# Both expert biases added by VectorE from tables picked by a register, where matmuls added them

## The chip, the cores and the metric

One core of one Trainium2 chip runs the whole program in one launch. The metric is the device time of that launch in microseconds (us); lower is better. A measurement is the median of several executions.

## What is computed

A decoder layer with three parts, each followed by an addition to its input and a layer norm: self-attention with a dynamic convolution, cross attention over 1601 context rows, and a mixture of experts, which is the part that changes. 4 x 512 tokens of width 256 each go to the best two of eight experts:

```python
logits = jnp.einsum('bsd,de->bse', input, Wg)
probs = jax.nn.softmax(logits, axis=-1)
top_vals, top_idx = jax.lax.top_k(probs, TOP_K)          # TOP_K = 2
top_vals = top_vals / jnp.sum(top_vals, axis=-1, keepdims=True)
...
h = jnp.einsum('ebsd,edh->ebsh', xm, W1) + b1[:, None, None, :]   # 256 -> 512
h = jax.nn.relu(h)
y = jnp.einsum('ebsh,ehd->ebsd', h, W2) + b2[:, None, None, :]    # 512 -> 256
out = jnp.sum(y * jnp.moveaxis(scores, -1, 0)[..., None], axis=0)
```

b1 is 8 x 512 and b2 is 8 x 256. Both are non-zero.

## The kernel before

The three parts run one behind the other, each in a block of its own with one hand-written instruction stream for each engine; semaphores set the order between engines, and the order within an engine is that of the code.

**Ahead.** The object `Ahead` loads what the experts need while the cross attention still runs: the gate's weights, the two biases (`b2_raw`, `b1c`) and the raw weights of experts 0 and 1, into two staging buffers (STG = 2). `Ahead.start` is the first thing that SyncE issues in the cross attention; behind it in the same queue stand the loads of the first batch's input, `xa_xh` and `xa_xl`, which TensorE needs for the first query projection.

**Gate and list.** TensorE computes the gate; VectorE picks the two experts of each token, ranks the 4096 assignments and builds a list of 39 blocks (NBK) of 128 rows, each of one expert: `gidx` and `sidx` say which rows to gather and where to scatter, `eidi` says which expert a block has. Its last step releases `list_ready`.

**Weights.** Each float32 weight is split in two parts. ScalarE writes w_hi (`take_weights`), GpSimd writes w_lo for experts 0, 1, 2, 5, 6, 7 and VectorE for 3 and 4 (`low_weights`). When w_lo of an expert is done, its staging buffer is free and SyncE loads the expert after next. Weights 0 to 4 are taken before the blocks, 5, 6 and 7 at blocks 1, 2 and 4.

**Blocks.** GpSimd gathers the rows of block q three blocks ahead and scatters the results. For one block TensorE turns the rows (`turn_x`, L1395), which are split into xb_hi (ScalarE) and xb_lo (VectorE); runs the first layer (L1409, six matmuls of 512 columns, and L1413, one for b1); turns h_f back (`turn_h`, L1420), which is split into h_hi and h_lo; and runs the second layer (L1427, one for b2, and L1431, twelve of 256 columns). Its order is first_layer(q), turn_x(q+1), second_layer(q-1), turn_h(q). The bias matmuls multiply `sel`, a 128 x 128 selector that ScalarE fills for each block (L1492) from `pick`, with `bx`, which holds both biases in two parts. `xb`, `h_f`, `h_hi`, `h_lo` and `sel` have two buffers each. TensorE reads the expert's number from `eidi` into a register (L1401) for the weights' address.

At the end the results come back from `ybuf`, are weighted, added and normalised.

## Time and profile before

| | us |
|---|---|
| median of 3 runs | 1970.57 |
| lowest and highest | 1967.91, 1973.7 |
| the profiled execution | 1969.15 |
| its span, first to last instruction | 1967.4 |
| TensorE busy in it | 1740.5 (88%) |
| VectorE, ScalarE, GpSimd busy | 1136.5, 864.6, 1290.6 |
| mean granted TensorE clock | 0.937 |

All times below are of the profiled execution, counted from its first instruction. Self-attention ends at about 210, the cross attention at about 1710, and the 39 blocks run from 1771 to 1930. Busy shares are means over stages with different limits, so the stages are read one by one: a row of idle time names what the engine waited for, and a DMA row of the timeline shows the time in issue, not in transfer.

### The profile page before, as it was taken

Reading aid. Unit: us, or ns where it says so; the run is one execution under the profiler, and the core shown is the slowest. Engines: PE = TensorE matmul, PEld = TensorE weight load, DVE = VectorE, ACT = ScalarE, POOL = GpSimd, SP = SyncE. Lnnn points to the kernel's source line nnn. Section 1 sums busy time; section 2 is a strip of 40 time slices with the busy share of each in tenths; the row PEclk is TensorE's granted clock in tenths of the full one; section 3 lists DMA queues with packets and bytes.
Section 4 is the critical chain, followed back from the end, with each engine's and each line's share of the span. In section 5 each row is a group of like instructions: output and inputs, shape, how many; then the busy total and the mean of one; then the engine's idle time right before and its main releaser. Section 6 shows DMA issues by size and latency. Waiting matters only on the chain. (4 is left out here: it accounts for less than half of the span.)

```text
span 1967.4 us, 32756 instructions
## 1 busy us (share of the span) xinstructions
PE 1740.5 (88%) x10682; PEld 1217.7 (62%) x10682; DVE 1136.5 (58%) x1993; ACT 864.6 (44%) x1280; POOL 1290.6 (66%) x721
## 2 busy tenths in 40 slices
PE   6554499999989999998999999989999998649992
PEld 5544366666656666665666666656666675347991
DVE  4776455556565656656565656566665555463444
ACT  3222244445444445444444444544544444334443
POOL 3874438677686676686866767677668677636554
PEclk9877699999999999999999999999999999759996
DMA  6001300000200000010000000200000000023224
GB/s 192 2 22 38 113 1 23 1 23 0 76 1 23 1 24 23 0 55 22 22 1 23 2 22 0 76 1 23 22 1 23 16 0 1 19 95 117 71 71 139
DMA packets 38854, 68.09 MB, mean 35 GB/s; under 512 B 4601, under 2 KB 28545, under 8 KB 37697
## 3 DMA queue, kind: packets, MB, share of 16 engines
q1 hardware_dynamic: 34976, 56.12, 8.5%
q0 software_dynamic: 3744, 10.23, 1.6%
q8 instruction: 80, 1.31, 0.3%
q14 instruction: 54, 0.43, 0.1%
HBM read 52.84 MB, written 13.50 MB: 34 GB/s over the span
## 5 line engine op out<-in xcount | busy, mean ns | idle before, releaser
L1034 POOL TENSOR_TENSOR xa_total<-xa_total,xa_pexp 128x1024 f32<-128x1024 f32 (+1 forms) x352 | 858.3, 2438 | 63.8 <-ACT xa_pexp L975 38.8
L1100 DVE TENSOR_REDUCE xa_parts<-ps_ring 128x1 f32<-128x402 f32 x1024 | 531.9, 565 | 267.4 <-PE ps_ring L920 253.7
L975 ACT ACTIVATE xa_pexp<-ps_s 128x1024 f32<-128x1024 f32 (+1 forms) x416 | 426.1, 1026 | 400.7 <-PE ps_s L875 361.6
L889 PE MATMUL ps_pv<-xa_pexp,xa_v 128*64 128x512 f32 (+1 forms) x1664 | 399.8, 604 | 0.0
L920 PE MATMUL ps_ring<-xa_k_hi,xa_q_hi 64*128 64x402 f32 x1024 | 245.1, 376 | 7.2 <-DVE xa_parts L1100 5.0
L889 PEld LDWEIGHTS ps_pv<-xa_pexp,xa_v 128*64 128x64 f32 (+1 forms) x1664 | 106.1, 136 | 181.9 <-issue 141.6
L875 PE MATMUL ps_s<-xa_q_hi,xa_k_hi 64*128 64x512 f32 (+1 forms) x832 | 203.1, 437 | 3.6 <-DVE xa_k_lo L1088 2.7
L1088 DVE TENSOR_TENSOR xa_k_lo<-ps_ring,xa_k_hi 128x402 fp32r<-128x402 f32 (+1 forms) x128 | 73.6, 575 | 218.8 <-ACT xa_k_hi L986 218.8
L920 PEld LDWEIGHTS ps_ring<-xa_k_hi,xa_q_hi 64*128 64x128 f32 x1024 | 149.6, 186 | 78.8 <-issue 23.3
L875 PE MATMUL ps_s<-xa_q_neg,xa_row_one 64*128 64x512 f32 (+1 forms) x832 | 180.8, 393 | 0.0
L1034 POOL TENSOR_TENSOR xa_total<-xa_pexp 128x1024 f32<-128x1024 f32 x32 | 76.4, 2387 | 158.9 <-ACT xa_pexp L975 157.5
L875 PE MATMUL ps_s<-xa_q_lo,xa_k_hi 64*128 64x512 f32 (+1 forms) x832 | 180.1, 393 | 0.0
L875 PE MATMUL ps_s<-xa_q_hi,xa_k_lo 64*128 64x512 f32 (+1 forms) x832 | 179.7, 392 | 0.0
L1010 ACT COPY xa_v<-ps_ring 128x256 f32<-128x256 f32 (+1 forms) x208 | 77.5, 373 | 184.6 <-PE ps_ring L860 182.7
L1115 DVE RECIPROCAL xa_inv<-xa_sums 128x128 f32<-128x128 f32 x128 | 120.0, 941 | 27.5 <-ACT xa_sums L997 27.5
L1056 POOL TENSOR_TENSOR xa_wa_lo<-wa_raw,xa_wa_hi 128x1536 fp32r<-128x1536 f32 x17 | 59.0, 3472 | 110.0 <-ACT xa_wa_hi L1020 110.0
L875 PEld LDWEIGHTS ps_s<-xa_q_hi,xa_k_hi 64*128 64x128 f32 (+1 forms) x832 | 82.6, 182 | 67.2 <-issue 40.3
L860 PEld LDWEIGHTS ps_ring<-xa_wa_hi,xa_ctx_hi 128*128 128x128 f32 (+1 forms) x416 | 62.3, 185 | 63.9 <-issue 60.9
L875 PEld LDWEIGHTS ps_s<-xa_q_neg,xa_row_one 64*128 64x128 f32 (+1 forms) x832 | 92.2, 181 | 14.3
L875 PEld LDWEIGHTS ps_s<-xa_q_lo,xa_k_hi 64*128 64x128 f32 (+1 forms) x832 | 91.8, 181 | 14.0
L1060 POOL TENSOR_TENSOR xa_wb_lo<-wb_raw,xa_wb_hi 128x512 fp32r<-128x512 f32 x16 | 22.0, 1376 | 116.3 <-ACT xa_wb_hi L1023 116.3
L986 ACT CAST xa_k_hi<-ps_ring 128x402 fp32r<-128x402 f32 (+1 forms) x128 | 63.3, 495 | 79.4 <-PE ps_ring L860 79.4
(272 smaller groups left out, 2956.0 us busy)
## 6 DMA issues: line engine op xcount, KB each, us to landing
wa_raw<-in_pack_a SPq DMA_DIRECT2D x17, 768.0 KB, 4.5
ex_raw<-in_pack_e SPq DMA_DIRECT2D x8, 1024.0 KB, 5.8
ctx_raw<-in_ctxT SPq DMA_DIRECT2D x4, 1601.0 KB, 8.7
wb_raw<-in_pack_b SPq DMA_DIRECT2D x16, 256.0 KB, 2.6
ex_w_hi<-ybuf SPq DMA_DIRECT2D x8, 512.0 KB, 7.3
sa_xT<-in_xT SPq DMA_DIRECT2D x8, 256.0 KB, 6.3
X<-in_x SPq DMA_DIRECT2D x1, 2048.0 KB, 11.1
x_hi<-sa_x1s_hi SPq DMA_DIRECT2D x16, 128.0 KB, 2.1
```

What stands on the lines that cost most here:

```text
L860: ins = nc.tensor.matmul(out, w, x, start=q == 0, stop=q == len(terms) - 1)
L875: ins = nc.tensor.matmul(ps_s[0:m, t_of(n), h, :], kk[half(h)], qq[half(h), :], start=q == 0, stop=q == 3)
L889: ins = nc.tensor.matmul(ps_pv[half(h), :], v[0:m, t, at:at + XD], pexp[0:m, buf, h, :], start=t == 0, stop=t == MT - 1)
L920: nc.tensor.matmul(ps_ring[:, r, 0:CW], q_hi[p][half(h), q * P:(q + 1) * P], k_hi[p][half(h), KC0[c]:KC0[c] + CW], start=True, stop=True)\
L975: nc.scalar.activation(pexp[0:m, buf], ps_s[0:m, (p * MT + t) % 2], ACT.Exp, scale=XD ** -0.5)\
L986: nc.scalar.copy(k_hi[p][:, KC0[c] + skip:KC0[c] + CW], ps_ring[:, r, skip:CW])\
L1010: nc.scalar.copy(v[0:rows(t), t, :], ps_ring[0:rows(t), r, 0:4 * XD]).then_inc(drained[r], 1)
L1034: nc.gpsimd.tensor_tensor(total[p][0:m], first, pexp[0:m, buf], ALU.add).then_inc(s["add_done"], 1)
L1056: nc.gpsimd.tensor_tensor(wa_lo[:], wa_raw[:], wa_hi[:].bitcast(F32), ALU.subtract)\
L1088: nc.vector.tensor_tensor(k_lo[p][:, cols], ps_ring[:, r, skip:CW], k_hi[p][:, cols].bitcast(F32), ALU.subtract).then_inc(drained[r], 1)
L1100: nc.vector.tensor_reduce(parts[:, h, q, c:c + 1], ps_ring[:, r, 0:CW], AX.X, ALU.max)\
L1115: nc.vector.reciprocal(inv[:, cs], sums[:, cs]).then_inc(s["inv_ready"], 1)
```

## The change

Both biases leave TensorE. Two tables hold them on all 128 partitions: `b1_all` (8 x 512 a partition) and `b2_all` (8 x 256). VectorE reads the block's expert into a register of its own and adds a row of the table as it drains PSUM: `take_h`, which was ScalarE's copy, and `take_y`, which was a copy of VectorE's. `sel`, `pick`, `bx` and their preparation go.

`b1_rows` is a new DRAM tensor with b1 in plain order; four DMAs in `Ahead.start` fill it from the packed weights, one number at a time. `b1_all` is loaded from it at the start of the experts. `b2_all` lies over tables of the gate and is loaded once the list is done; the loads of experts 4 to 7 stand behind it in SyncE's order. `xb_hi`, `xb_lo`, `h_f`, `h_hi` and `h_lo` have one buffer instead of two, and the gate's tables share their room with the blocks'. The second layer now starts when h_hi is done and waits for h_lo before its last third.

```diff
     def start(self, sp, a):
         sp.dma_start(self.wg[:], a["Wg"].rearrange("(k p) e -> p k e", p=P)).then_inc(self.sems["small_in"], 16)
-        sp.dma_start(self.b2_raw[:], a["b2"]).then_inc(self.sems["small_in"], 16)
-        sp.dma_start(self.b1c[:], a["pack_e"][:, :, WW:].rearrange("e p c -> p e c")).then_inc(self.sems["small_in"], 16)
+        for c in range(HC):
+            sp.dma_start(self.b1_rows.rearrange("o (e c p) -> (o e) c p", e=NE, c=HC)[:, c], a["pack_e"][:, :, WW + c], allow_slow_non_contiguous=True)\
+                .then_inc(self.sems["rows_in"], 16)
         for e in range(STG):
             self.load(sp, a, e)
...
         @block.sync
         def _(sp):
+            sp.wait_ge(ahead.sems["rows_in"], 16 * HC)
+            sp.dma_start(b1_all[:].rearrange("p e n -> p (e n)"), ahead.b1_rows.broadcast_to([P, NE * HID]))\
+                .then_inc(s["b1_in"], 16)
             for b in range(B):
                 sp.wait_ge(s["x_done"], NC * (b + 1))
...
-            for e in range(STG, NE):
+            for e in range(STG, STG + 2):
+                lo_done(sp, e - STG + 1)
+                ahead.load(sp, a, e)
+            sp.wait_ge(s["list_ready"], 1)
+            sp.dma_start(b2_all[:].rearrange("p e n -> p (e n)"),
+                         a["b2"].rearrange("(o e) n -> o (e n)", o=1).broadcast_to([P, NE * E])).then_inc(s["b2_in"], 16)
+            for e in range(STG + 2, NE):
                 lo_done(sp, e - STG + 1)
                 ahead.load(sp, a, e)
...
-                pe.wait_ge(s["sel_done"], q + 1)
-                nc.tensor.matmul(ps_h[:, q % 2, :], sel[:, q % 2], bx[:, 0:HID], start=False, stop=True)\
-                    .then_inc(s["h_mm"], 1)
...
             def second_layer(q):
                 e = experts_of[q]
-                pe.wait_ge(s["h_done"], q + 1)
+                pe.wait_ge(s["h_hi_done"], q + 1)
                 need(pe, s["y_copied"], q - 1)
-                nc.tensor.matmul(ps_y[:, q % 2, 0:E], sel[:, q % 2], bx[:, HID:HID + E], start=True, stop=False)
                 terms = [(h, w, c) for h, w in ((h_hi, w_hi), (h_hi, w_lo), (h_lo, w_hi)) for c in range(HC)]
                 for n, (h, w, c) in enumerate(terms):
+                    if n == 2 * HC:
+                        pe.wait_ge(s["h_done"], q + 1)
...
             def take_x(q):
                 act.wait_ge(s["xb_tr"], q + 1)
-                need(act, s["h_mm"], q - 1)
-                nc.scalar.copy(xb_hi[:, q % 2], ps_x[:, q % 2, 0:E]).then_inc(s["xb_hi_done"], 1)
-                need(act, s["y_mm"], q - 1)
-                nc.scalar.copy(sel[:, q % 2], pick[:, q:q + 1].bitcast(F32).broadcast_to([P, P])).then_inc(s["sel_done"], 1)
-
-            def take_h(q):
-                act.wait_ge(s["h_mm"], q + 1)
-                need(act, s["h_tr"], q - 1)
-                nc.scalar.copy(h_f[:, q % 2], ps_h[:, q % 2]).then_inc(s["h_copied"], 1)
+                need(act, s["h_mm"], q)
+                nc.scalar.copy(xb_hi[:], ps_x[:, q % 2, 0:E]).then_inc(s["xb_hi_done"], 1)
...
+            def take_h(q):
+                e = dve.value_load(eidi[0:1, q:q + 1], min_val=0, max_val=NE - 1)
+                experts_of[q] = e
+                dve.wait_ge(s["h_mm"], q + 1)
+                need(dve, s["h_tr"], q)
+                nc.vector.tensor_tensor(h_f[:], ps_h[:, q % 2],
+                                        b1_all[:, bass.ds(e, 1), :].rearrange("p a n -> p (a n)"), ALU.add)\
+                    .then_inc(s["h_copied"], 1)
...
-                nc.vector.tensor_copy(y_sb[:, q % 3], ps_y[:, q % 2, 0:E]).then_inc(s["y_copied"], 1)
-
+                nc.vector.tensor_tensor(y_sb[:, q % 3], ps_y[:, q % 2, 0:E],
+                                        b2_all[:, bass.ds(experts_of[q], 1), :].rearrange("p a n -> p (a n)"), ALU.add)\
+                    .then_inc(s["y_copied"], 1)
+
+            dve.wait_ge(s["b1_in"], 16)
             take_x(0)
             for q in range(NBK):
+                take_h(q)
                 if q + 1 < NBK:
                     take_x(q + 1)
```

SyncE, at the start of the cross attention, before (a row gives the line, the tensors and the shape; b_raw is b2_raw):

```order
L738 DMA ex_wg<-in_Wg 128x2x8
L739 DMA ex_b_raw<-in_b 8x256
L740 DMA ex_b1c<-in_pack_e 128x8x4
L735 DMA ex_raw<-in_pack_e 128x2048 x2
L844 DMA xa_xh<-x_hi 128x1024
L844 DMA xa_xl<-x_lo 128x1024
```

The same place in the changed kernel (b_rows is b1_rows):

```order
L740 DMA ex_wg<-in_Wg 128x2x8
L742 DMA b_rows<-in_pack_e 8x128x1 x4
L737 DMA ex_raw<-in_pack_e 128x2048 x2
L847 DMA xa_xh<-x_hi 128x1024
L847 DMA xa_xl<-x_lo 128x1024
```

The b2 and b1c loads have gone, and four DMAs of 8 x 128 x 1 stand in their place, ahead of the same four loads.

SyncE, from the start of the experts to the return of the results, in the changed kernel (both tables are named ex_b_all; the first is b1_all, the second b2_all):

```order
L1255 DMA ex_b_all<-b_rows 128x4096
L1259 DMA x<-X 128x4x256 x4
L737 DMA ex_raw<-in_pack_e 128x2048 x2
L1265 DMA ex_b_all<-in_b 128x2048
L737 DMA ex_raw<-in_pack_e 128x2048 x4
L1275 DMA ex_w_hi<-ybuf 128x4x256 x8
```

Before, this was the stores of x2 and six weight loads (x6) in a row; now the loads of experts 4 to 7 stand behind b2_all.

VectorE, one block in the steady state, before:

```order
L1660 TENSOR_TENSOR ex_xb_lo<-ps_x,ex_xb_hi 128x256
L1674 COPY ex_y_sb<-ps_y 128x256
L1666 SCALAR_TENSOR_TENSOR ex_h_lo<-ps_t,ex_h_hi 128x512
L1660 TENSOR_TENSOR ex_xb_lo<-ps_x,ex_xb_hi 128x256
L1674 COPY ex_y_sb<-ps_y 128x256
```

And in the changed kernel (TENSOR_LOAD reads the register, ISA rows are register work):

```order
L1645 SCALAR_TENSOR_TENSOR ex_h_lo<-ps_t,ex_h_hi 128x512
L1652 TENSOR_LOAD ex_eidi
L1652 ISA x2
L1656 ISA
L1656 TENSOR_TENSOR ex_h_f<-ps_h,ex_b_all 128x512
L1639 TENSOR_TENSOR ex_xb_lo<-ps_x,ex_xb_hi 128x256
L1666 ISA
L1666 TENSOR_TENSOR ex_y_sb<-ps_y,ex_b_all 128x256
```

The register load and the drain of the first layer stand between h_lo of one block and xb_lo of the next.

## Rows read from the trace of the kernel before

**Rows 1.** The page, busy tenths of TensorE in 40 equal slices of the span.

```profile
PE   6554499999989999998999999989999998649992
```

**Rows 2.** Timeline, TensorE, 195 to 260: start, length, line, tensors, [idle before, releaser].

```profile
229.91 1.22 PE L860 MATMUL ps_ring<-xa_xh,xa_wa_hi 128*128 128x512 f32 x2 [4.75 <-DMA xa_xl<-x_lo]
```

**Rows 3.** Timeline, SyncE's queue, 195 to 245: start and length of the issue.

```profile
213.42 0.41 SPq L740 DMA_DIRECT2D ex_b1c<-in_pack_e  x1
...
214.96 4.27 SPq L844 DMA_DIRECT2D xa_xh<-x_hi  x1
```

**Rows 4.** DMA in 214:217, 217:221 and 215:216; then windows, whose last columns are share and GB/s.

```profile
DMA packets 682, 0.01 MB, mean 4 GB/s; under 512 B 680, under 2 KB 682, under 8 KB 682
...
DMA packets 415, 0.73 MB, mean 181 GB/s; under 512 B 327, under 2 KB 327, under 8 KB 327
...
DMA packets 325, 0.01 MB, mean 5 GB/s; under 512 B 325, under 2 KB 325, under 8 KB 325
...
214.00:217.00 3.00, 0.00 (x0) 0.00 (x0) 2.92 (x2) 3.00 (x3) 2.93 (x1) 0.50 0.11 4
...
222.00:228.00 6.00, 2.35 (x6) 1.83 (x6) 1.29 (x2) 0.49 (x1) 6.00 (x3) 0.50 1.01 415
```

**Rows 5.** Timelines of ScalarE, VectorE and TensorE, 1740 to 1772.

```profile
1748.18 1.90 ACT L1455 CAST ex_w_hi<-ex_raw 128x2048 fp32r<-128x2048 f32 x1 [4.51 <-DMA ex_raw<-in_pack_e]
...
1765.06 0.17 DVE L1646 TENSOR_SCALAR ex_gidx<-ex_wrap 128x39 uint32<-128x39 f32 x1
...
1766.31 4.49 DVE L1558 TENSOR_TENSOR ex_w_lo<-ex_raw,ex_w_hi 128x2048 fp32r<-128x2048 f32 x2
...
1771.39 1.22 PE L1409 MATMUL ps_h<-ex_w_hi,ex_xb_hi 128*128 x2 [1.47 <-DVE ex_xb_lo L1660]
```

**Rows 6.** The tile ex_raw, its eight loads from issue to landing.

```profile
DMA to landing us min/median/max: 4.8/5.8/12.9
```

**Rows 7.** Timeline, all engines, 1851.3 to 1863: one steady block.

```profile
1852.07 0.69 DVE L1666 SCALAR_TENSOR_TENSOR ex_h_lo<-ps_t,ex_h_hi 128x512 fp32r<-128x512 f32 x1 [0.64 <-ACT ex_h_hi L1502]
...
1852.61 0.40 PE L1413 MATMUL ps_h<-ex_bx,ex_sel 128*128 128x512 f32 x1
...
1852.85 0.38 PE L1395 MATMUL ps_x<-ident,ex_xg 128*128 128x128 f32 x2
...
1852.98 0.36 PE L1427 MATMUL ps_y<-ex_bx,ex_sel 128*128 128x256 f32 x1
...
1853.18 0.64 PE L1431 MATMUL ps_y<-ex_w_hi,ex_h_hi 128*128 x4
...
1854.60 0.60 PE L1420 MATMUL ps_t<-ident,ex_h_f 128*128 128x128 f32 x4
...
1855.87 0.69 DVE L1666 SCALAR_TENSOR_TENSOR ex_h_lo<-ps_t,ex_h_hi 128x512 fp32r<-128x512 f32 x1 [0.64 <-ACT ex_h_hi L1502]
```

**Rows 8.** Groups by form, 1811.65 to 1923.02: busy, mean ns of one, idle before.

```profile
L1497 ACT COPY ex_h_f<-ps_h 128x512 f32<-128x512 f32 x30 | 17.6, 588 | 30.6 <-PE ps_h L1413 30.6
...
L1413 PE MATMUL ps_h<-ex_bx,ex_sel 128*128 128x512 f32 x29 | 11.4, 394 | 0.0
```

**Rows 9.** The chain that ended last, 1780 to 1794: start, length, what.

```profile
1780.96 1.90 ACT ex_w_hi L1455
1782.94 4.64 POOL ex_w_lo L1300
1787.72 5.55 DMA ex_xg<-x,ex_gidx
```

**Rows 10.** The chain that ended last, at the last block.

```profile
1927.85 0.70 DVE ex_h_lo L1666
...
1928.60 0.39 PE ps_y L1427
1928.98 1.42 PE ps_y L1431 x12
```

**Rows 11.** TensorE's queue at the register load: ns min, median, max.

```profile
L1401 PEldq TENSOR_LOAD <-ex_eidi x39: 296/302/497, 1769.3 to 1922.2; - x39
```

## What the change should do to the time

> **What bounds the kernel now.** I read the slices of the page first: TensorE is at nine tenths or more through the cross attention, from a tenth of the span to nine tenths of it, and falls off on both sides of that stretch [rows 1]. The change touches nothing inside the stretch, but it touches both of its edges, so I read three places: the DMA queue at the start of the cross attention, the gap between the finished list and the first expert block, and the 39 blocks.
>
> At the start of the cross attention the reader is to see that TensorE has stood still for 4.75 us when it goes on at 229.91, and that what it waited for is the DMA that brings xa_xl [rows 2]. From there on TensorE is nearly full, so whatever delays that DMA delays the end by the same amount. It is the last of seven DMAs that SyncE issues in a row, and its predecessor xa_xh stands 4.27 us in issue: the queue is backed up [rows 3]. The packets tell why. From 214 to 217 the engines are 11% busy and move 4 GB/s in 680 packets under 512 bytes, 327 more follow to 221, and only then does the flow reach 415 GB/s [rows 4]. Those 1007 packets are b1c: 128 x 8 pieces of 16 bytes = 1024.
>
> In the blocks, TensorE has no idle time between 1811 and 1923 (the group at L1413 shows 0.0 of it, as do its others), and a block repeats every 3.80 us, 1852.07 to 1855.87 at the h_lo step [rows 7, 8]. The blocks before that are set by another chain: ScalarE w_hi, GpSimd w_lo, then the gather queued behind it, 1780.96 to 1793.32 and once more to 1807 [rows 9].
>
> **The tiny DMAs at the start of the cross attention.** Removed: one of 8 rows (b2) and b1c with 1024 pieces of 16 bytes. Added: four DMAs from DRAM to DRAM, each 8 x 128 x 1, so 4 x 1024 = 4096 pieces of 4 bytes, in the same place of the same queue, ahead of the two raw loads and of xa_xh and xa_xl. No row shows a 4-byte piece written to DRAM. The nearest row is b1c itself. Its pieces take from 214.0 until the large packets have the engines, about 220.5: 6.5 us, or 6.3 ns a piece. 4096 of them take 26.0 us, which is 19.5 more. The low end is the best stretch of the same pieces: 680 in 3 us is 4.4 ns, so 18.0 - 4.5 = 13.5 more, and if the fastest microsecond, 325 packets, held throughout, 3.1 ns and 9.4 more [rows 4]. Below nothing it can't go: more pieces of the same kind in one queue don't end sooner. The high end is double the time of a piece, 52 - 6.5 = 45.5, for the reason given as a rival. I take **+19.5**, since it is the row's own average, head and tail included. Cover: none. TensorE waits for xa_xl already, and ScalarE, VectorE and GpSimd don't stand in that wait.
>
> The count of 4096 is the shape's, as 1007 of 1024 was b1c's. The Trainium skill says the same (DMA: Bandwidth & Descriptors, "Rules for kernel authors"): a non-contiguous last dimension becomes one descriptor per element. It adds, in "Specifications", that under 512 bytes the engine reads, modifies and writes; no row here prices that for a DRAM target. Both speak against this change, and neither enters the sum.
>
> **The new table loads.** b1_all (2 MB, issued at about 1711) lies ahead of the stores of x2, which are needed only at the gathers, after 1765.23; at 415 GB/s it is gone in 5 us: nothing. Without that cover it would cost those 5. b2_all is another matter. SyncE now waits for the finished list before it issues b2_all, and the load of expert 4 is queued behind it. Before, expert 4's weights had landed by 1748.18, when ScalarE copied them, long before the list (1765.06 + 0.17 = 1765.23) [rows 5]. Now both DMAs start at about 1765.1. One load lands 4.8 us after issue at best; the second 1 MB behind it adds 2.6 at 400 GB/s, and three gathers of 128 KB beside them 1.0 [rows 4, 6]. So expert 4 lands at 1773.5. Behind it stand, in order, w_hi on ScalarE (1.90), w_lo on VectorE (half of 4.49, 2.25) and take_x(0) on VectorE (0.35): TensorE starts block 0 at about 1778.4 where it started at 1771.39 [rows 5, 6]. That is **+7.0**; the two bias rows of VectorE that go (1765.26 to 1766.31) gain nothing, being hidden by this wait. Bounds: +5.9 without the gathers' share, +10 if the load takes the 12.9 of the slowest raw load in the trace. The loads of 5 and 6 follow in the same queue: 5 lands by about 1776 and 6 by 1783, and ScalarE wants them 6 us later than 1780.96 and 1784.8, so they have 8 us to spare.
>
> **The blocks.** L1413 goes: from its start to the next start, 1852.61 to 1852.85, 0.24 us. L1427 goes: 1852.98 to 1853.18, 0.20, of which some is weight load that the next matmul may have to pay; an L1431 step is 0.118 (twelve in 1.42), so 0.12 to 0.20, and I take 0.16 [rows 7, 10]. Blocks 8 to 38 are bound by TensorE: 31 x 0.24 + 32 x 0.16 = **-12.5** (-11.3 to -13.8). Before them, in the two blocks at the slow clock ahead of the w_hi chain, go 0.44 (L1413 at half the clock, so a little under twice its 0.24), 0.24 and 0.2, less 0.1 for the slower drain of h_f, and 0.3 for L1427 at half the clock in block 4: **-1.1** [rows 7]. At the end, the last second layer starts behind h_hi instead of h_lo, whose 0.70 now lies under the first eight matmuls (8 x 0.118), and L1427's 0.39 go: **-1.0** [rows 10].
>
> Does what replaces them stay covered? h_f moves from ScalarE (0.588) to VectorE, where a 128x512 read of PSUM with a second operand takes 0.69 [rows 7, 8]. Counted from the start of a turn_h (1850.80, by the period, to the h_lo at 1852.07): VectorE ends h_lo at 1.96, the next first layer has ended by about 2.0, h_f is done at 2.7, and the next turn_h is due only at 3.4 [rows 7]. The register load ahead of it costs TensorE's queue 302 ns today [rows 11]; on VectorE it stands behind h_lo's issue, under its 0.69. Even if it began only when h_lo has ended, h_f would be done at 3.0 and take_x (0.42) behind it at 3.5, before the 3.76 at which the next first layer is due. The skill gives a floor of about 600 ns for tensor_load (same page, "Latency and other measured facts"); the trace has 302, and the trace decides. Single buffers cost nothing: every wait that they add is for a step of TensorE that its own order already puts ahead. VectorE's work rises to 0.69 + 0.69 + 0.42 + 0.42 = 2.2 us of a 3.4 us block, ScalarE's falls.
>
> **Sum:** 19.5 + 7.0 - 12.5 - 1.1 - 1.0 = +11.9 on the profiled execution's 1969.15, which is 1981.0. That execution lies 1.4 under the median of the three, 1970.57, so by the median **1982.5**, say 1983.
>
> **Rivals.** (1) The pieces take twice as long, because the four new DMAs have 8 rows outermost where b1c has 128, and are spread over half of the 16 engines. For it: b1c's pieces leave the engines 11% busy, so something other than data holds them, and that may be a latency per ring. 64 pieces on each of 16 rings in 6.5 us are 0.10 us each; 512 on each of 8 rings are 52 us: +45.5 at the start, 2009 in all. Against it: the pace of b1c jumps within microseconds, which a fixed latency doesn't explain. The Trainium skill (same page, "Why a DMA increments its semaphore by 16 and not by 1") says that a DMA uses the largest number of engines up to 16 that divides its slowest dimension, which is 8 here and 16 for b1c. (2) The other side, **faster**: the pieces are overtaken or pass at several times b1c's pace. For it: nothing forces the raw loads on idle engines to wait. The blocks' gain nets 7.6 after expert 4's wait, so it decides once the start costs less than 7.6; at no cost the time is 1963. Against it: xa_xh stood 4.27 us in issue behind a quarter of the pieces. (3) The start costs the low bounds, 9.4 to 13.5: 1972 to 1976. (4) The register load and the address work behind it take three times TensorE's 302 ns on VectorE, and begin only behind h_lo: 1.96 + 0.9 + 0.69 + 0.42 = 3.97 against 3.76, 0.1 to 0.2 in each of 31 blocks, so +3 to +6 on the forecast, 1986 to 1989.
>
> **How the numbers follow.** A measurement of this kernel can tell about 0.3%, 5.9 us, from no change: under 1964.7 is faster, over 1976.5 slower. Forecast (and 4 within it) 0.50, rival 1 0.23, rival 3 0.15, rival 2 0.12. Slower: 0.73; within: 0.16; faster: 0.11. The range runs from rival 3 with the other terms at their low ends (9.4 + 5.9 - 13.8 - 2.1 = -0.6, 1970) to rival 1, 2010, and leaves out rival 2 and a tail above.
>
> **What would show it.** TensorE's wait for xa_xl should grow from 4.75 to about 24 us, with some 4350 packets under 512 bytes ahead of it; 50 would be rival 1, 5 rival 2. Expert 4's w_hi should start 8 to 9 us after the list instead of 17 before it, and the first block 13.3 us after it instead of 6.2. Steady blocks should repeat every 3.40 us instead of 3.79; 3.5 would be rival 4. The forecast is wrong above all if a 4-byte piece doesn't cost what a 16-byte piece did.

## The result

The changed kernel takes 2015.0 us (median of 4 runs, 2011.5 to 2015.8) where the kernel before takes 1971.7 (4 runs, 1967.9 to 1973.7): a ratio of 1.0223, 95% interval 1.021 to 1.0235. It is slower by 43 us, and the time lies 5 us above the range that was forecast. The profiled execution took 2015.17 us, with a span of 2013.4; before, 1969.15 and 1967.4.

I lay the two spans side by side at five events that both kernels have. All times are starts unless an end is named, in us from the start of the span; the last two columns are a later experiment, explained below.

| event | before | after | later by | `e12_b2_late` | later by |
|---|---|---|---|---|---|
| first statistics of the expert stage (VectorE) | 1711.35 | 1760.38 | +49.0 | 1706.97 | -4.4 |
| list finished (end of `gidx`) | 1765.23 | 1814.23 | +49.0 | 1761.26 | -4.0 |
| block 0, first layer | 1771.39 | 1826.85 | +55.5 | 1768.33 | -3.1 |
| `turn_x(8)` | 1807.26 | 1863.86 | +56.6 | 1803.49 | -3.8 |
| end of the span | 1967.4 | 2013.4 | +46.0 | 1953.1 | -14.3 |

So 49.0 us were lost before the experts began, 6.5 between the list and block 0, 1.1 in the first eight blocks, and 10.6 were won back by the blocks behind them.

**The start of the cross attention.** The slices of the page show it at once: one slice is 50 us, and TensorE's fifth, at 4 tenths before [rows 1], is empty now.

```profile
PE   6655049999999999999999999999999999646992
```

The timeline of TensorE in the changed kernel (start, length, line, tensors, [idle before, releaser]) is the counterpart of [rows 2]: it goes on at 280.41 instead of 229.91.

```profile
280.41 1.22 PE L863 MATMUL ps_ring<-xa_xh,xa_wa_hi 128*128 128x512 f32 x2 [54.80 <-DMA xa_xl<-x_lo]
```

SyncE's queue in the changed kernel (start and length of the issue), the counterpart of [rows 3], shows what stands ahead of that DMA. The four table DMAs alone hold the queue for 28.81 us, and xa_xl is issued at 252.47.

```profile
213.41 28.81 SPq L742 DMA_DIRECT2D b_rows<-in_pack_e  x4
242.27 6.58 SPq L737 DMA_DIRECT2D ex_raw<-in_pack_e  x2
248.90 3.53 SPq L847 DMA_DIRECT2D xa_xh<-x_hi  x1
252.47 0.88 SPq L847 DMA_DIRECT2D xa_xl<-x_lo  x1
```

The packets of the changed kernel in 214:220, 220:230, 230:240, 240:250 and 250:260, the counterpart of [rows 4]:

```profile
DMA packets 1484, 0.02 MB, mean 4 GB/s; under 512 B 1483, under 2 KB 1483, under 8 KB 1483
...
DMA packets 600, 0.00 MB, mean 0 GB/s; under 512 B 600, under 2 KB 600, under 8 KB 600
...
DMA packets 96, 0.00 MB, mean 0 GB/s; under 512 B 96, under 2 KB 96, under 8 KB 96
...
DMA packets 1724, 0.06 MB, mean 6 GB/s; under 512 B 1717, under 2 KB 1717, under 8 KB 1717
...
DMA packets 529, 0.28 MB, mean 28 GB/s; under 512 B 495, under 2 KB 495, under 8 KB 495
```

They add up to 4391 small packets; the count was forecast (4350). The pace was not: after 1483 in the first 6 us it breaks down, and in ten whole microseconds 96 pass.

**Expert 4 and block 0.** The counterpart of [rows 5], timelines of the changed kernel from 1812 to 1827:

```profile
1814.06 0.17 DVE L1630 TENSOR_SCALAR ex_gidx<-ex_wrap 128x39 uint32<-128x39 f32 x1
...
1814.26 0.33 SPq L1265 DMA_DIRECT2D ex_b_all<-in_b  x1
...
1822.04 1.90 ACT L1456 CAST ex_w_hi<-ex_raw 128x2048 fp32r<-128x2048 f32 x1 [28.63 <-DMA ex_raw<-in_pack_e]
...
1823.97 2.29 DVE L1545 TENSOR_TENSOR ex_w_lo<-ex_raw,ex_w_hi 128x2048 fp32r<-128x2048 f32 x1 [7.54 <-ACT ex_w_hi L1456]
...
1826.85 1.22 PE L1415 MATMUL ps_h<-ex_w_hi,ex_xb_hi 128*128 x2 [2.92 <-DVE ex_xb_lo L1639]
```

The reader sees the chain that the prediction wrote down: the load lands, ScalarE copies w_hi 7.8 us behind the list, VectorE makes w_lo, then xb_lo, and block 0 starts 12.6 us behind the list, where it was 6.2. But the first gather is late too: `turn_x(0)`, which uses its rows, starts at 1823.27, 9.0 us behind the list, and before at 1769.26, 4.0 behind it.

**A steady block.** Timelines of TensorE and VectorE in the changed kernel, the counterpart of [rows 7]:

```profile
1877.81 0.38 PE L1401 MATMUL ps_x<-ident,ex_xg 128*128 128x128 f32 x2
1877.95 0.72 PE L1436 MATMUL ps_y<-ex_w_hi,ex_h_hi 128*128 x4
...
1878.12 0.69 DVE L1656 TENSOR_TENSOR ex_h_f<-ps_h,ex_b_all 128x512 f32<-128x512 f32 x1 [0.18 <-PE ps_h L1415]
...
1878.50 0.63 PE L1436 MATMUL ps_y<-ex_w_lo,ex_h_hi 128*128 x4
...
1879.44 0.60 PE L1424 MATMUL ps_t<-ident,ex_h_f 128*128 128x128 f32 x4
...
1881.58 0.69 DVE L1656 TENSOR_TENSOR ex_h_f<-ps_h,ex_b_all 128x512 f32<-128x512 f32 x1 [0.18 <-PE ps_h L1415]
```

A block now takes 3.46 us (1878.12 to 1881.58) where it took 3.79 to 3.80. TensorE shows no idle time in it, and h_f is done at 1878.81, 0.63 us before `turn_h` starts: VectorE is off the path, though by less than these 0.63, as `e7_all_mended` will show. The register load on VectorE's queue (columns: ns min, median, max) costs what it costs TensorE [rows 11]:

```profile
L1652 DVEq TENSOR_LOAD <-ex_eidi x39: 300/305/551, 1824.5 to 1971.2; - x39
```

### The profile page after: what moved, and what is told of

It reads as the page before. It is cut to its first block and busy times, and to the rows that moved or that the text cites. A ratio compares the mean times of both kernels' runs of the same rounds, so it can differ in the third digit from the quotient of the medians.

```text
span 2013.4 us, 32750 instructions
## 1 busy us (share of the span) xinstructions
PE 1731.5 (86%) x10600; PEld 1210.5 (60%) x10600; DVE 1158.5 (58%) x2026; ACT 831.6 (41%) x1199; POOL 1291.1 (64%) x720
## 6 DMA issues: line engine op xcount, KB each, us to landing
wb_raw<-in_pack_b SPq DMA_DIRECT2D x16, 256.0 KB, 2.6
sa_xT<-in_xT SPq DMA_DIRECT2D x8, 256.0 KB, 6.1
```

## The experiments

Thirteen kernels ran. A ratio is always to runs of the kernel before on the same chip; medians of different runs are compared across chips and carry some us of doubt.

### Where the 50 us at the start come from

The first batch leaves the tables as they are and moves or reshapes the pieces that make them.

**The order alone.** `e1_rows_behind` issues the same four DMAs behind xa_xl.

```diff
     def start(self, sp, a):
         sp.dma_start(self.wg[:] ...
-        for c in range(HC):
-            sp.dma_start(self.b1_rows...[:, c], a["pack_e"][:, :, WW + c], ...)
...
                         sp.dma_start(dst[:].bitcast(F32), src[bass.ds(next_batch(i), 1)] ...   # xa_xh, xa_xl
+                    if n.prologue:
+                        ahead.fill_rows(sp, a)      # the same four DMAs
```

> The changed kernel with the four b1 DMAs issued behind xa_xl instead of ahead of the raw loads; nothing else differs. If the 50 us are the wait of TensorE for xa_xl behind these pieces, that wait falls from 54.8 us to below the 4.75 us of the kernel before (b1c's pieces are gone too, so 0 to 2 us), and the time falls by 50 to 56 us, to about 1960 to 1965. Rival: the pieces cost the same wherever they stand, because the next loads (wb_raw, wa_raw) queue behind them and TensorE then waits for those weights; then the wait moves to a later place and the time stays over 1990.

Measured: 1964.3 us (8 runs, 1961.8 to 1979.5), 0.9984 of the kernel before (0.9955 to 1.0013), so not to be told from it. Against the 2015.0 of the changed kernel that is 50.8 us by the medians and 47 by the ratios and by the profiled spans (2013.4 and 1966.4), for the order of a few DMAs: the start term is the pieces' place in SyncE's queue. The pieces themselves are no cheaper there, as SyncE's queue of this kernel and its one new stand of TensorE show:

```profile
214.16 34.35 SPq L741 DMA_DIRECT2D b_rows<-in_pack_e  x4
...
253.34 17.16 SPq L838 DMA_DIRECT2D wa_raw<-in_pack_a  x1
...
282.58 0.79 PE L882 MATMUL ps_s<-xa_q_lo,xa_k_hi 64*128 64x512 f32 x2 [5.00 <-issue]
```

The weights of the next head start to issue 25 to 29 us later than before (wb_raw at 248.55 instead of 223.87, wa_raw at 253.34 instead of 224.24), and TensorE shows no wait for them. TensorE stands once, for 5.00 us, in the middle of a group of matmuls and with no releaser in the trace. No packet under 512 bytes moves in that stand (276 to 282.6 has 37 packets, all larger, at 32 GB/s), so the tiny pieces themselves are over by then; what it is stays open. In the profiled run the experts begin at 1713.11, 1.8 us later than before, though the wait of 4.75 is gone; the stand is the one part of that loss that a row shows.

**Number, shape and target of the pieces.** Four kernels change the pieces in their old place, and one gives the kernel before pieces like them.

```diff
 e2_half_pieces    (half of the b1 table is left out: c = 0, 1 only)
-        for c in range(HC):
+        for c in range(HC // 2):
...
 e3_128_rows       (same pieces, the 128 hidden units outermost on both sides)
-  b1_rows "o (e c p) -> (o e) c p" [:, c]   <-  pack_e[:, :, WW + c]
+  b1_rows "o (e c p) -> (o p) e c" [:, :, c]   <-  pack_e[:, :, WW + c] "e p -> p e"
...
 e4_sbuf_target    (same pieces into SBUF, 8 rows outermost; the store to DRAM follows at the experts' start)
+  b1_sb[c * NE:(c + 1) * NE]   <-  pack_e[:, :, WW + c]
...
 e5_16_bytes       (DRAM to DRAM, 1024 pieces of 16 bytes; take_h reads the row with a stride of 4)
+  b1_rows "o (e p c) -> (o e) p c"   <-  pack_e[:, :, WW:WW + HC]
...
 e8_before_4_bytes (the kernel before; b1c in 4 x 1024 pieces of 4 bytes, 128 outermost, into SBUF)
+        for c in range(HC):
+            sp.dma_start(self.b1c[:, :, c], a["pack_e"][:, :, WW + c].rearrange("e p -> p e"), ...)
```

> The changed kernel with two of the four b1 DMAs (2048 pieces of 4 bytes instead of 4096); both halves of the table are then loaded from these, so half of b1 is wrong. If the cost goes by the number of pieces, TensorE's wait for xa_xl falls from 54.8 to 54.8 - 28 = about 27 to 30 us. If it is a fixed stall that any such DMA brings (a full queue, the ten empty us seen at 230 to 240), it stays above 40.

> The changed kernel with the same 4096 pieces of 4 bytes, DRAM to DRAM, but each DMA walks 128 x 8 x 1 instead of 8 x 128 x 1. Rings theory (rival 1 of the prediction: latency per piece and ring, 8 of 16 rings in use): the wait for xa_xl falls from 54.8 to about 27 to 30 us. Count theory (one generator or one common path sets the pace): it stays at 50 to 55.

> The changed kernel with the same four DMAs of 8 x 128 x 1 pieces of 4 bytes, but written to SBUF (32 rows of 512 bytes, stored to DRAM as rows later, at the start of the experts). DRAM-write theory: what is dear is a 4-byte write into DRAM; then the wait for xa_xl falls from 54.8 to 15 to 25 us, b1c's pace times four. Rings or count theory: the target doesn't matter, 50 to 55.

> The changed kernel with b1_rows filled by one DMA of 1024 pieces of 16 bytes, DRAM to DRAM, in the order expert, p, c (the drain then reads the table with a stride of four). Piece theory (the cost goes by pieces on a ring, whatever their bytes, and a DRAM target about doubles it): 64 pieces a ring, a quarter of the 256 a ring of the run with 128 rows, whose wait was 28.0 us: the wait for xa_xl is 4.75 to 10 us. Byte theory (4 bytes are dear because they are smaller than what DRAM writes at once, 16 are not): the same or a little less, 3 to 5 us, so this run mostly shows that the shape mends it; total about 1970 either way. If the strided read of the table costs VectorE more than 0.3 us a block, the steady block grows over 3.46.

> The kernel before with its own b1c load cut into four DMAs of 128 x 8 x 1: 4096 pieces of 4 bytes, 16 rings, SBUF target. It is the fourth corner beside 8 rings to DRAM (wait 54.8), 16 rings to DRAM (28.0) and 8 rings to SBUF (19.6). If rings and target act apart, each by a factor, the wait for xa_xl is about 10 to 12 us. If SBUF pieces are held by one common path (count theory for SBUF), it is 19 to 20, as with 8 rings; the prediction's own pace of 6.3 ns a piece would give 24.

Measured, by TensorE's wait for xa_xl in each timeline, in the order e2, e3, e4, e5, e8:

```profile
249.16 1.22 PE L863 MATMUL ps_ring<-xa_xh,xa_wa_hi 128*128 128x512 f32 x2 [24.10 <-DMA xa_xl<-x_lo]
...
253.90 1.22 PE L863 MATMUL ps_ring<-xa_xh,xa_wa_hi 128*128 128x512 f32 x2 [27.96 <-DMA xa_xl<-x_lo]
...
243.13 1.22 PE L863 MATMUL ps_ring<-xa_xh,xa_wa_hi 128*128 128x512 f32 x2 [19.60 <-DMA xa_xl<-x_lo]
...
229.14 1.22 PE L862 MATMUL ps_ring<-xa_xh,xa_wa_hi 128*128 128x512 f32 x2 [5.43 <-DMA xa_xl<-x_lo]
...
244.54 1.22 PE L862 MATMUL ps_ring<-xa_xh,xa_wa_hi 128*128 128x512 f32 x2 [19.18 <-DMA xa_xl<-x_lo]
```

| pieces ahead of xa_xl | outermost | target | wait for xa_xl, us | total, us |
|---|---|---|---|---|
| 1024 x 16 bytes (before) | 128 | SBUF | 4.75 | 1971.7 |
| 1024 x 16 bytes (e5) | 8 as written | DRAM | 5.43 | 1978.2 |
| 4096 x 4 bytes (e8) | 128 | SBUF | 19.18 | 1987.8 |
| 4096 x 4 bytes (e4) | 8 | SBUF | 19.60 | 1977.9 |
| 2048 x 4 bytes (e2) | 8 | DRAM | 24.10 | 1982.5 |
| 4096 x 4 bytes (e3) | 128 | DRAM | 27.96 | 1987.0 |
| 4096 x 4 bytes (after) | 8 | DRAM | 54.80 | 2015.0 |

(e2, e3, e4, e5 and e8 are one run each; e8 is the kernel before but for b1c, so its total lacks what the change does in the blocks, and the waits are what is to be compared.) Three things follow. The wait grows with the number: from 2048 to 4096 pieces it rises by 30.7 us, 15.0 ns a piece. The shape counts only when the pieces are written to DRAM: 8 outermost instead of 128 costs 26.8 us there, and nothing in SBUF (19.60 against 19.18, in two otherwise different kernels). And 1024 pieces of 16 bytes cost nearly the same into either memory (4.75 and 5.43). Of these shapes only small, many and 8 outermost into DRAM together make the 54.80.

The Trainium skill (DMA: Bandwidth & Descriptors, "Why a DMA increments its semaphore by 16 and not by 1") says that a DMA is spread over the largest number of engines, up to 16, that divides the slowest dimension of both its sides: by that rule 8 for the changed kernel's pieces, 16 for e3's. The factor of two between 54.80 and 27.96 agrees with that; the SBUF pair, 8 and 16 by the same rule, shows no such factor.

One rival to the number of engines was not tried. With 8 outermost, pieces that follow each other are written to neighbouring 4 bytes of `b1_rows`; e3 also turns that order, so that they lie 2 KB apart. Which of the two, the engines or the order of the writes, gives the factor of two stays open.

**Are the 4.75 us of before made by pieces at all?** The forecast took its price from that wait. `e13_before_b1c_behind` moves b1c behind xa_xl in the kernel before.

```diff
-        sp.dma_start(self.b1c[:], a["pack_e"][:, :, WW:].rearrange("e p c -> p e c")) ...   # in start
...
+                    if n.prologue:
+                        ahead.fill_rows(sp, a)      # the same DMA, behind xa_xl
```

> The kernel before with its b1c load (1024 pieces of 16 bytes) issued behind xa_xl instead of ahead of it; nothing else changes. Theory A, that the 4.75 us for which TensorE stands for xa_xl in the kernel before are these pieces: the wait is gone and the total is some 4 to 5 us lower, about 1966 us. Then some 4.5 of the 14 us by which e12_b2_late beats the kernel before owe nothing to the biases. Theory B, that the wait is the landing time of xa_xl itself (1 MB issued late behind the two expert loads): it stays at 4 us or more and the total at 1970 us; then the price of 6.3 us ns a piece in the forecast was taken from a wait that pieces did not make.

Measured: 1964.6 us (10 runs), ratio 0.9978 (0.9965 to 0.999), and of the wait 0.20 is left:

```profile
225.75 1.22 PE L864 MATMUL ps_ring<-xa_xh,xa_wa_hi 128*128 128x512 f32 x2 [0.20 <-DMA xa_xl<-x_lo]
```

Theory A holds: the pieces made the wait. They made 4.55 us of it, though, and not the 6.5 us that the forecast took for 1024 pieces: 4.4 ns a piece instead of 6.3. For 4 bytes into SBUF (e8) the same division, 19.18 less the 0.20 that stay without pieces, gives 4.6 ns. So a 4-byte piece costs what a 16-byte piece does as long as it goes to SBUF; into DRAM it is 6.8 ns in e3 and 13.3 in the changed kernel.

### Expert 4's load

`e6_load4_first` issues the load of expert 4 before SyncE waits for the list.

```diff
-            for e in range(STG, STG + 2):
+            for e in range(STG, STG + 3):
...
-            for e in range(STG + 2, NE):
+            for e in range(STG + 3, NE):
```

> The changed kernel with the load of expert 4 issued ahead of the wait for the list and b2_all, as in the kernel before. Expectation: block 0 starts 5 to 6.2 us after the list instead of 12.6 (1814.23 to 1826.85), so 6.4 to 8 us earlier, and the whole is 2015.0 - 7 = about 2008. Rival: the gathers or w_lo set block 0 anyway, and the gain is under 3 us. If TensorE's clock rises earlier with it, the ramp before block 8 shortens from 37.0 to about 35 us as well; if it doesn't, the slow clock comes from the gaps inside block 0 and 1 themselves.

Measured: 2007.2 us (2 runs), ratio 1.0187 (1.0167 to 1.0207), 7.9 under the changed kernel by the medians and 6.7 by the profiled spans. 2.4 of that is a shorter wait for xa_xl in this run (52.39), which the edit can't have made. Timelines of this kernel around block 0:

```profile
1811.44 0.17 DVE L1630 TENSOR_SCALAR ex_gidx<-ex_wrap 128x39 uint32<-128x39 f32 x1
...
1819.93 0.66 PE L1401 MATMUL ps_x<-ident,ex_xg 128*128 128x128 f32 x2 [10.33 <-DMA ex_xg<-x,ex_gidx]
...
1821.84 1.22 PE L1415 MATMUL ps_h<-ex_w_hi,ex_xb_hi 128*128 x2 [1.24 <-DVE ex_xb_lo L1639]
```

Block 0 starts 10.2 us behind the list: 2.4 of the 6.5 come back, not all. What is late next is the first gather, issued at 1812.52 and used at 1819.93, 7.4 us later, beside two loads of 1 MB: b2_all, issued at 1811.64 and landed 4.7 us later, and behind it expert 5's weights, issued at 1813.89 and landed 5.7 us later. Before, the gather was used 3.1 us after its start (1766.14 to 1769.26), with no large load beside it until 1768.68. The eight blocks of the ramp take 35.2 us here (1821.84 to 1856.99) against 37.0 in the changed kernel.

### All of it together, and a surprise

`e7_all_mended` puts e5's 16-byte pieces behind xa_xl and takes e6's edit as well; its diff is those two.

> The changed kernel with all three: 16-byte pieces, issued behind xa_xl, and the load of expert 4 ahead of b2_all. If the accounts hold: 2015.0 - 50.5 (wait for xa_xl back to that of before) - 5.4 (the wait of before, 4.75, goes too) - 7 (expert 4) = about 1952, so 0.990 to 0.991 of the kernel before, faster by a measurable amount. Rival: part of the start is given back later, as in the run with the 4096 pieces behind xa_xl, where TensorE stood 5.0 us at 277.6; then 1955 to 1960.

Measured: 1969.6 us (12 runs), ratio 0.9998 (0.9989 to 1.0006). The start is mended (no wait for xa_xl) and so is expert 4, yet the gain of the blocks is gone. The group of h_f's addition in the changed kernel (busy, mean ns of one, idle before) and in this one, over the steady blocks:

```profile
L1656 DVE TENSOR_TENSOR ex_h_f<-ps_h,ex_b_all 128x512 f32<-128x512 f32 x30 | 20.7, 692 | 6.6 <-PE ps_h L1415 6.6
```

```profile
L1659 DVE TENSOR_TENSOR ex_h_f<-ps_h,ex_b_all 128x512 f32<-128x512 f32 x30 | 32.3, 1076 | 15.8 <-PE ps_h L1418 15.8
```

With 16-byte pieces the table has the four columns of a hidden unit side by side, and the addition reads its row with a stride of four. That takes 1.08 us instead of 0.69, and h_f stands between the first layer and `turn_h`. VectorE's timeline of this kernel:

```profile
1850.83 1.07 DVE L1659 TENSOR_TENSOR ex_h_f<-ps_h,ex_b_all 128x512 f32<-128x512 f32 x1 [0.53 <-PE ps_h L1418]
...
1854.62 1.08 DVE L1659 TENSOR_TENSOR ex_h_f<-ps_h,ex_b_all 128x512 f32<-128x512 f32 x1 [0.52 <-PE ps_h L1418]
```

A block takes 3.79 us (1850.83 to 1854.62), just what it took before the change. So 0.33 of the 0.38 us come through, although in the changed kernel h_f was done 0.63 us before `turn_h` started. Here h_f ends at 1851.90, `turn_h` still follows its predecessor closely (1852.14), but the next first layer has an idle time of 0.30 us ahead of it, put down to issue:

```profile
1852.14 0.60 PE L1427 MATMUL ps_t<-ident,ex_h_f 128*128 128x128 f32 x4
...
1852.81 0.31 PEld L1418 LDWEIGHTS ps_h<-ex_w_hi,ex_xb_hi 128*128 128x128 f32 x2 [0.30 <-issue]
```

In TensorE's stream the register load of the next block stands directly behind `turn_h`. The rows of `eidi` over one block alone give the single load (ns min, median and max, then its start), first in the changed kernel and then in this one:

```profile
L1407 PEldq TENSOR_LOAD <-ex_eidi x1: 304/304/304, 1878.9 to 1878.9; - x1
```

```profile
L1410 PEldq TENSOR_LOAD <-ex_eidi x1: 301/301/301, 1852.0 to 1852.0; - x1
```

In both it starts 0.1 us after h_f has ended (1878.81, 1851.90), so the queue passes `turn_h` when h_f is done and not when `turn_h` starts.

From the end of h_f to the first weight load of the next first layer it is 0.91 us here (to 1852.81); 0.30 of that is the load, and what fills the rest the trace doesn't name. In the changed kernel the same stretch was 0.96 (to 1879.77), with TensorE busy. So the real slack there was 0.05 us and not 0.63, and an addition that is 0.38 longer comes through with 0.33. The one block of `e11_plain_rows` below whose plain addition was late (1844.59, 0.69 long) shows the 0.91 as well, with 0.24 of idle time. e5 has the same stride and the same 0.91, and its additions take 1.07 to 1.08 us too. The stride is what its total and e7's have in common: from block 0 to the end it is 197.2 us in e5 against 186.6 in the changed kernel, and 195.0 in e7 against 184.9 in e6, so the stride costs 10.2 to 10.6 us.

### One matmul at a time

`e9_no_b2_matmul` and `e10_no_b1_matmul` are the kernel before without L1427 and without L1413; each leaves that bias out of the result.

```diff
 e9:
-                nc.tensor.matmul(ps_y[:, q % 2, 0:E], sel[:, q % 2], bx[:, HID:HID + E], start=True, stop=False)
...
 e10:
-                nc.tensor.matmul(ps_h[:, q % 2, :], sel[:, q % 2], bx[:, 0:HID], start=False, stop=True)
```

> The kernel before without the matmul of L1427 (the second bias is left out of the result; sel, bx and all else stay). It splits the 0.33 us that a steady block gained. Theory A, the matmul takes its whole 0.16 us: 38 x 0.16 = -6.1 us, a steady block of 3.63 us, about 1964 us. Theory B, as the trace of the changed kernel suggests (there the first four matmuls of L1436 take 0.55 us from start to start where they took 0.48 behind L1427): most of it is given back, a steady block of 3.69 to 3.71 us, -3.0 to -3.8 us, about 1967.

> The kernel before without the matmul of L1413 (the first bias is left out of the result; the wait for sel_done stays). Theory A: a steady block loses its 0.24 us, 3.55 us, 39 x 0.24 = -9.4 us, about 1961 us. Theory B, that this matmul was partly hidden too: 3.60 us or more, 1963 us or later.

Measured, one run each beside a median of 1970.9 for the kernel before (1968.7 to 1974.8): 1967.4 and 1967.4. Differences of that size in a single run prove little, so the steady block is what is read. TensorE's steady block in e9, then in e10:

```profile
1850.15 0.60 PE L1420 MATMUL ps_t<-ident,ex_h_f 128*128 128x128 f32 x4
...
1852.35 0.72 PE L1430 MATMUL ps_y<-ex_w_hi,ex_h_hi 128*128 x4
1852.90 0.63 PE L1430 MATMUL ps_y<-ex_w_lo,ex_h_hi 128*128 x4
...
1853.85 0.60 PE L1420 MATMUL ps_t<-ident,ex_h_f 128*128 128x128 f32 x4
```

```profile
1850.80 0.60 PE L1419 MATMUL ps_t<-ident,ex_h_f 128*128 128x128 f32 x4
...
1852.63 0.38 PE L1395 MATMUL ps_x<-ident,ex_xg 128*128 128x128 f32 x2
1852.82 0.38 PE L1426 MATMUL ps_y<-ex_bx,ex_sel 128*128 128x256 f32 x1
...
1854.45 0.27 PE L1419 MATMUL ps_t<-ident,ex_h_f 128*128 128x128 f32 x1
```

Without the b2 matmul a block takes 3.70 us: theory B. The 0.20 that L1427 occupied are gone, but the first four matmuls of the second layer take 0.55 from start to start where they took 0.48. Without the b1 matmul it takes 3.65, and theory B again: 0.24 are gone, and the two transposes behind it hold the engine for 0.19 where they held it for 0.13, and L1427 behind them for 0.22 where it was 0.20, so 0.15 is left. Alone they are worth 0.10 and 0.15, together 0.33 to 0.34. The parts don't add up because what each short matmul covers of its neighbour depends on the other: with both gone, in the changed kernel, the two transposes take 0.14 again (1877.81 to 1877.95) and there is no L1427 to pay 0.02 more.

### A version that keeps the gain

`e11_plain_rows` fetches b1 behind xa_xl in 16-byte pieces into SBUF, turns it into plain rows there with one GpSimd copy (32 x 128, 0.40 us), stores it in runs of 128 bytes and broadcasts it as the changed kernel does; expert 4 loads first. `e12_b2_late` also holds b2_all back until the first gather has landed.

```diff
+        for u in range(4):          # behind xa_xl
+            sp.dma_start(self.b1_nc[NE * u:NE * (u + 1)]..., a["pack_e"][:, 32 * u:32 * (u + 1), WW:WW + HC])
...
+            nc.gpsimd.tensor_copy(ahead.b1_cn[:].rearrange("e (c p) -> e c p", c=HC),
+                                  ahead.b1_nc[:].rearrange("e (p c) -> e c p", c=HC))
...
             sp.wait_ge(s["list_ready"], 1)
+            sp.wait_ge(g_in[0], 16)     # e12 only
             sp.dma_start(b2_all[:] ...
```

> The changed kernel with the b1 rows fetched behind xa_xl in pieces of 16 bytes into SBUF, brought into the plain order there by one small copy on GpSimd, stored in 128-byte runs and broadcast as before, and with expert 4's load ahead of b2_all. VectorE's addition reads plain rows again. Theory A, that the stride of four in the table is what kept e7_all_mended at 1969.6: its steady block there is 3.80 us and here 3.46, so 39 x 0.34 = -13.3 us, about 1956 us. Theory B, that something else eats the gain (the start, the ramp): 1965 us or more. The first gather still shares the DMA engines with b2_all, so block 0 should start some 10 us behind the list, as in e6_load4_first.

> As e11_plain_rows, but b2_all is issued only when the first gather has landed. Theory A, that b2_all is what made that gather land after 7.3 us: block 0 starts about 6.2 us behind the list, as in the kernel before, 4 us earlier than in e11_plain_rows, and the total is about 1952 us. Theory B, that the gather is slow for another reason (expert loads): block 0 stays at 10 us behind the list and nothing changes. Theory C: b2_all now comes too late for the first result (it is needed some 9 us behind block 0's first copy), and the wait moves to L1666.

Measured: 1958.2 us (4 runs), ratio 0.9935 (0.9916 to 0.9953), and 1955.8 us (4 runs), ratio 0.9922 (0.9904 to 0.9941). Both beat the kernel before. e11 is 11.4 us under e7 by the medians, where 13.3 were expected, and its addition takes 0.69 us again; not all of the 11.4 need be the stride, since e11's experts begin 4.1 us earlier and its clock rises later than e7's. e12 against e11, around block 0 (e11's two rows, then e12's):

```profile
1758.14 0.17 DVE L1641 TENSOR_SCALAR ex_gidx<-ex_wrap 128x39 uint32<-128x39 f32 x1
...
1768.55 1.22 PE L1426 MATMUL ps_h<-ex_w_hi,ex_xb_hi 128*128 x2 [1.24 <-DVE ex_xb_lo L1650]
```

```profile
1761.09 0.17 DVE L1642 TENSOR_SCALAR ex_gidx<-ex_wrap 128x39 uint32<-128x39 f32 x1
...
1766.43 0.66 PE L1413 MATMUL ps_x<-ident,ex_xg 128*128 128x128 f32 x2 [7.19 <-DMA ex_xg<-x,ex_gidx]
...
1768.33 1.22 PE L1427 MATMUL ps_h<-ex_w_hi,ex_xb_hi 128*128 x2 [1.24 <-DVE ex_xb_lo L1651]
```

Block 0 starts 10.2 us behind the list in e11 and 7.1 in e12; 6.2 was hoped for. The gather is used 4.3 us after its start (1762.16 to 1766.43) instead of 7.4. So the large loads beside it slowed it, but e12 holds back two of them, b2_all and, behind it in the queue, expert 5's weights; which of the two did it was not tried apart. Against the 3.1 us of before 1.2 are left unexplained. e12 gains more than that: its clock is up 4 us behind block 0 and the first results are scattered 8.9 us behind it, against 9 and 11.0 in e11. Still the median is only 2.4 lower, since in e11 the list was finished 3.0 us earlier, which this edit has no part in. Of e12's 14.3 us of span, the table of the result gives 4.4 to the start, which e13 reaches without touching the biases (ratio 0.9978), and 10.5 to the blocks from the ninth on. The whole change, mended and with the order of e12, is worth the distance between 0.9978 and 0.9922, about 11 us; the two intervals allow 5 to 17. From the start of the experts to the end the profiled runs give 9.9 (246.1 against 256.0).

## Why the prediction was wrong, step by step

The direction was right, the size was not: +43 us against +12.

- **What bounds the kernel; where to look.** Right. All that moved lies at the start, at expert 4 and in the blocks, and TensorE's wait for xa_xl is paid nearly in full at the end: TensorE goes on 50.5 us later than before, and 49.0 are left when the experts begin.
- **The tiny DMAs, +19.5: the step that failed.** The wait grew from 4.75 to 54.80, and TensorE went on 50.5 us later. That the wait of before was made by pieces was right (e13), and so was the count (4391 packets). The price of 6.3 ns was that of a 16-byte piece into SBUF with 128 rows outermost, and it was put on a 4-byte piece into DRAM with 8 outermost, where a piece takes 13.3. Even for SBUF it was too high: the wait gives 4.4 to 4.6 ns there (e13, e8). With 128 outermost into DRAM the wait is 27.96, near the 24 that I forecast, but that is luck: the high price made up for the dearer target. The shape that e3 changes is what doubled it. That was rival 1 by its size, with its 50 us and its 2009; its reason, half of the engines, agrees with e3 and isn't shown. I gave it 0.23 because b1c's pace within the trace spoke against a latency per ring. That argument was read from pieces that go to SBUF, and for those e4 and e8 bear it out: they show no effect of the outermost dimension. It says nothing of a DRAM target, which no row showed. With a term of that size and no row for it, the two prices should have had equal chances, and the range a longer upper end: its end had rival 1's double price and nothing above it.
- **Expert 4, +7.0.** It measured +6.5, along the chain that was written down, but the agreement is in part luck. With expert 4 out of the way block 0 still starts 10.2 us behind the list (e6), so only 2.4 of the 6.5 are expert 4's own and 4.1 the late gather takes by itself. The forecast costed three gathers beside b2_all at 1.0 us; the first one takes 8.1 us in the changed kernel (1815.14 to 1823.27) and 7.4 in e6, instead of 3.1.
- **The ramp, -1.1.** It measured +1.1. TensorE's clock was to rise as before, and did not. The windows of the changed kernel and then of the kernel before (busy time of each engine, granted clock, DMA share, GB/s):

```profile
1832.00:1834.00 2.00, 2.00 (x6) 1.52 (x6) 0.69 (x1) 0.42 (x1) 0.00 (x0) 0.50 0.20 66
1834.00:1836.00 2.00, 2.00 (x11) 1.80 (x10) 1.12 (x2) 0.37 (x1) 0.00 (x0) 0.57 0.00 0
```

```profile
1776.00:1778.00 2.00, 2.00 (x10) 1.53 (x9) 0.81 (x2) 0.60 (x1) 0.47 (x1) 0.98 0.68 262
```

  In the changed kernel the granted clock is still 0.50 (1.2 GHz) 7 us behind block 0's start at 1826.85; before, it stood at 0.98 some 5 us behind 1771.39. Ahead of block 0 TensorE had stood 11.05 and then 2.92 us, before 5.17 and 1.47. From block 0 to the first scatter of results it takes 10.75 us instead of 9.35 (1826.85 to 1837.60, 1771.39 to 1780.74). In e6, with stands of 10.33 and 1.24, it takes 8.84 (to 1830.68). That looks as if the second stand, the one for expert 4, went with the late clock, but e11 speaks against it: its stands are 10.36 and 1.24, as in e6, and it takes 10.98 (1768.55 to 1779.53), with the clock still low in a window that ends 9.4 us behind block 0:

```profile
1776.00:1778.00 2.00, 2.00 (x11) 2.00 (x10) 1.12 (x2) 0.37 (x1) 0.00 (x0) 0.52 0.00 0
```

  What sets the moment at which the clock rises stays open here; the runs with the late clock lose 1.4 to 2.1 us by the first scatter. Behind the first scatter GpSimd's chain of w_lo and gathers sets the pace, 26.5 us before and 26.3 after, so the matmuls that go there bring nothing that the rows show.
- **The blocks and the tail, -12.5 and -1.0.** Together they measured -10.6. The mechanism was right (TensorE binds them, VectorE stays covered, single buffers show no wait), and the size was off: 0.33 a block instead of 0.40. The cover was thinner than forecast: it was counted to the start of `turn_h`, with 0.7 us to spare, and the next first layer leaves only 0.05 (e7). The removed steps were taken from start to start, 0.24 and 0.16 to 0.20, but 0.07 of them comes back in the neighbouring matmul; e9 and e10 show each giving part of itself back.
- **Rival 4, the register load on VectorE.** It did not happen, though its sign, a block of 3.5 us, is nearly what was measured (3.46): the load takes 305 ns, starts at 1877.3 beside h_lo (1877.24) and is hidden. The Trainium skill gives about 600 ns as the floor (same page, "Latency and other measured facts"); both engines of this kernel show half of that.

## What to carry to other kernels

Price a DMA of tiny pieces by their number, by where they are written and by their shape, not by its bytes, and take a price only from a row that agrees in all three; if there is none, give the worst case an equal chance and put such a DMA behind everything that an engine waits for. A load that is moved behind a wait moves whatever is queued behind it, and the next transfer to be late may be one that shares the engines with it. When a fast step becomes strided or changes engine, look at the slack of its consumer's queue in the steady block: here the layout that cured the start lost about 10 us in the blocks.

## What was not expected of the hardware

- 4096 pieces of 4 bytes, DRAM to DRAM with 8 outermost, make the wait for a later DMA of the same queue 50.1 us longer than 1024 pieces of 16 bytes into SBUF. With 128 outermost it is 23.2 us more, into SBUF 14.4 to 14.9 in either shape. The stream is not even: 96 pieces from 230 to 240 and 1717 from 240 to 250. What holds it in between stays open.
- A VectorE addition of 128 x 512 float32 from PSUM takes 0.69 us with a plain second operand in SBUF and 1.08 with a stride of four.
- Three 128 KB gathers beside a 1 MB broadcast load and a 1 MB weight load: the first is usable after 7.4 us; after 4.3 with both loads held back (e12), and after 3.1 in the kernel before.
- The stand of 5.00 us in the middle of a matmul group in e1, behind 4096 tiny pieces, has no releaser in the trace. Its cause was not tried.
- With the same two stands ahead of block 0, the granted clock of TensorE rose 4 to 5 us behind it in e6 and 9 us behind it in e11.
